# In each unit of a fused attention: the scores of the next unit first, the maxima of five units ahead behind them

## The reference

```python
mod = silu(c) @ w_ada + b_ada                     # six vectors: shift, scale, gate, twice
h = norm(x) * (1 + scale) + shift
q, k, v = split(h @ w_qkv + b_qkv)                # 16 heads of 9 dimensions
attn = softmax(q @ k.T / sqrt(9))                 # 128 x 128 for each head and sequence
x = x + gate * (attn @ v @ w_proj + b_proj)
x = x + gate2 * mlp(norm(x) * (1 + scale2) + shift2)
```

## Time and profile before

| | |
|---|---|
| three runs | 1516.69, 1521.12, 1522.37 us |
| profiled execution | 1514.8 us, span of the trace 1512.9 us |
| mean granted TensorE clock | 0.977 |
| L648, maxima (x2048) | 122.2 us busy, 53.8 us idle before it |
| L666 and L670, scores (x4096) | 331.5 us busy, 3.5 us idle before them |
| L1259, exponential (x256) | 262.4 us busy, 1025 ns each |
| L1567, reduction (x256) | 310.8 us busy, 1214 ns each, 90.4 us idle before it |

### The profile page before, as it was taken

The page is one execution under the profiler, slowest core; times in us unless marked ns, Lnnn a source line. Parts: engine busy times, 40 slices in busy tenths (PEclk is TensorE's granted clock), DMA queues, the critical chain, the costliest instruction groups (busy, mean ns, idle before and its releaser), DMA issues. The chain is left out here.

```text
span 1512.9 us, 41073 instructions
## 1 busy us (share of the span) xinstructions
PE 1400.6 (93%) x16016; PEld 1047.5 (69%) x16016; DVE 1022.3 (68%) x2537; ACT 780.3 (52%) x1290; POOL 570.0 (38%) x771
## 2 busy tenths in 40 slices
PE   5799998999999999999998878887999999998998
PEld 2377776777777776777776666665776677676776
DVE  4688885766776767888546698886446666665342
ACT  2377764333333336776645466665554455564543
POOL 3355542211131213554324455653425243433222
PEclk9799999999999999999999999999999999998999
DMA  4755641111122033555000443453216766674111
GB/s 128 160 152 150 163 103 54 52 45 45 37 61 76 9 106 80 147 145 135 18 32 25 123 106 90 119 124 88 47 28 104 112 107 126 129 123 92 33 48 48
DMA packets 209129, 134.94 MB, mean 89 GB/s; under 512 B 142461, under 2 KB 191320, under 8 KB 202730
## 3 DMA queue, kind: packets, MB, share of 16 engines
q1 hardware_dynamic: 188978, 129.74, 35.7%
q10 hardware_dynamic: 19960, 2.57, 1.2%
HBM read 98.24 MB, written 33.24 MB: 87 GB/s over the span
## 5 line engine op out<-in xcount | busy, mean ns | idle before, releaser
L1567 DVE TENSOR_REDUCE negm<-banks 128x8 bf16<-128x1024 f32 x256 | 310.8, 1214 | 90.4 <-PE banks L648 89.5
L1259 ACT ACTIVATE prob<-banks 128x1024 f32<-128x1024 f32 x256 | 262.4, 1025 | 147.1 <-PE banks L670 143.8
L2031 POOL TENSOR_TENSOR X<-X,gx 128x288 f32<-128x288 f32 x128 | 104.1, 826 | 261.7 <-DVE gx L1597 259.9
L1393 ACT ACTIVATE hid<-banks 128x512 f32<-128x512 f32 x144 | 85.9, 597 | 219.9 <-PE banks L960 219.9
L976 PEld LDWEIGHTS banks<-wfc,hid 128*128 128x128 f32 x1152 | 156.7, 190 | 32.3 <-issue 20.1
L648 PE MATMUL banks<-qk 54*128 54x128 bf16 (+1 forms) x2048 | 122.2, 240 | 53.8 <-DVE negm L1567 23.0
L666 PE MATMUL banks<-qk 54*128 54x128 bf16 (+1 forms) x2048 | 167.4, 234 | 3.5 <-ACT prob L1259 1.7
L670 PE MATMUL banks<-mT,identb 64*128 64x128 bf16 x2048 | 164.1, 223 | 0.0
L976 PE MATMUL banks<-wfc,hid 128*128 128x144 f32 x1152 | 161.6, 286 | 2.1 <-DVE hid L1767 2.1
L648 PEld LDWEIGHTS banks<-qk 54*128 54x128 bf16 (+1 forms) x2048 | 69.6, 101 | 128.4 <-issue 68.5
L959 PE MATMUL banks<-hT,wfc 128*128 128x512 f32 x288 | 148.6, 597 | 1.0 <-DVE hid L1479 0.5
(11 more groups left out here) (172 smaller groups left out, 2778.5 us busy)
## 6 DMA issues: line engine op xcount, KB each, us to landing
qk<-qk_scr SPq DMA_DIRECT2D x96, 216.0 KB
gbuf<-gate_scr SPq DMA_DIRECT2D x64, 288.0 KB, 4.5
qk_scr<-parts SPq DMA_DIRECT2D x48, 288.0 KB, 2.8
qk<-qk_scr SPq DMA_DIRECT2D x96, 144.0 KB
qk<-cw_scr SPq DMA_DIRECT2D x8, 1024.0 KB, 4.9
qk_scr<-parts SPq DMA_DIRECT2D x48, 144.0 KB, 2.4
qk<-qk_scr SPq DMA_DIRECT2D x96, 72.0 KB
qk<-tok_scr SPq DMA_DIRECT2D x32, 216.0 KB
```

The lines of the kernel that those rows point to most:

```text
L1259: act.activation(prob[:, 2 * (U % 3):2 * (U % 3) + 2, :], pairs[1][:], ACT.Exp, scale=scale).then_inc(a_exp, 1)
L1567: dve.tensor_reduce(negm[:, u // 2, :, 4 * (u % 2):4 * (u % 2) + 4], pairs[0][:].rearrange("q s (h k) -> q s h k", k=T), AX.X, ALU.max, ne ...
```

## The change

In every unit of the attention the call of `scores(l, U + 1)` now stands ahead of `scores_for_max(l, U + AHEAD)`. The opening of a layer (`start_layer` and the units that the MLP issues) is as it was, and so is every other engine's program.

```diff
                     for u in range(UNITS):
                         U = UNITS * n + u
+                        if U + 1 < last:
+                            scores(l, U + 1)
                         if U + AHEAD < last:
                             scores_for_max(l, U + AHEAD)
-                        if U + 1 < last:
-                            scores(l, U + 1)
                         if u % 2 == 1 and U + 3 < last:
```

## The result

The changed kernel takes 1513.61 us in the median of 22 runs (1501.99 to 1521.99), the kernel before 1520.45 us in as many (1510.81 to 1531.23). The ratio is 0.9943 with a 95% interval of 0.9925 to 0.9961: 8.7 us faster, 5.9 to 11.4 (the medians differ by 6.8 us, the means by 8.1). The forecast was 3.6 us faster, 1517.5 us, range 1507 to 1525. The time lies in the range; the gain is about twice the forecast one.

What follows compares the result with a forecast made beforehand. TensorE, busy 93% of the span, was taken as the bound, so only its waits or slowed time could be won. +4.0 - 3.9 - 2.3 - 1.4 = -3.6 us, from the 1521.12 us median to 1517.5, range 1507 to 1525.

Steps and rivals of the forecast that it cites:

- The split into chains: TensorE's waits: maxima to maxima gain nothing; landing or other part to maxima shrink, maxima to other part grow, up to 0.56 us.
- Rival 1: All layers: every wait ahead of the maxima is hidden, -16 us, 1505 us; chance 0.15.
- Rival 3: Late maxima lose 6.7 us in layers 0 and 1 and 3.4 in layer 2, no gain: +10, 1531 us; chance 0.08.
- Rival 4: Whole kernel: the reordering does nothing anywhere, 1521 us; chance 0.10.
- Layers 0 and 1: forecast +4.0 us: Late unit 4 maxima delay a group's head transpose, 6.7 us lost; DMA waits return 1.4 and 1.3.
- the term of 12 x 0.56 = 6.7: Layers 0 and 1: twelve groups without slack each lose 0.56 us at the transpose waiting for GpSimd's copy.
- Layer 2: forecast -3.9: Scores run inside unit 3's DMA waits: six groups 0.56 us shorter each, 3.4, and 0.5 in the first group.
- clock term: Layer 2: shorter DMA waits may remove two clock drops of 1.4 us each; half counted, -1.4 us.
- The direct term: Layer 2: the gain from shorter DMA waits without the clock, 0.56 us a group, -3.9 us in all.
- Layer 3: forecast -2.3: Four DMA waits ahead of the maxima each shrink by up to 0.82 us: 0.8 from the longest, 1.5 from the others.
- The wait term: Layer 3: the gain from four shorter DMA waits, -2.3 us, with no clock drops counted.
- Rival 2: The clock decides: all four drops after waits vanish, -5.6 instead of -1.4 us, 1513 us; chance 0.12.

Runs made afterwards that it cites:

- e6_only6: Scores ahead of the maxima only in unit 6 of each group, against the kernel before: 1521.82 us, ratio 1.0007 (0.9985 to 1.0030).
- e5_only4: Scores ahead of the maxima only in unit 4 of each group, against the kernel before: 1525.94 us, ratio 1.0035 (1.0014 to 1.0055).
- e1_layers01: Scores ahead of the maxima only in layers 0 and 1, against the kernel before: 1522.86 us, ratio 1.0013 (0.9995 to 1.0030).
- e3_unit3: Scores ahead of the maxima only in unit 3 of each group, against the kernel before: 1515.10 us, ratio 0.9957 (0.9935 to 0.9980).
- e2_layers23: Scores ahead of the maxima only in layers 2 and 3, against the kernel before: 1511.98 us, ratio 0.9934 (0.9912 to 0.9956).
- e9_whole: The whole change once more, against the kernel before on the same chip: 1511.50 us, ratio 0.9956 (0.9936 to 0.9976).
- e7_best: Scores first everywhere but in unit 4 of layers 0 and 1, against the kernel before: 1511.43 us, ratio 0.9951 (0.9929 to 0.9972).

## Why the prediction was right, and what was mis-sized

**The split into chains held.** A wait between two groups of maxima gives nothing (e6_only6; in unit 6 it is there in both orders, 0.42 and 0.32 us from start to start), a chain from the maxima to another part of the stream costs (e5_only4, e1_layers01), one from a landing to the maxima gives (e3_unit3's 6.79 us for 7.26). Rival 1, every wait hidden, is refused by e1_layers01 and e6_only6. Rival 3, slower, came true only as its first half, in layers 0 and 1. Rival 4 is out by the interval. That the total fell inside the range is in part luck: the terms missed by -2, +1.5 and -4 us.

**Layers 0 and 1: forecast +4.0 us, measured +2.0 (e1_layers01; -0.8 to +4.6), by the stages 2.8 - 0.7.** The lateness is 0.47 us and not 0.56, and a group grows by 0.37 to 0.40 us (22.47 to 22.84 in layer 0, 22.30 to 22.70 in layer 1), since VectorE makes up some 0.08 of it. So the term of 12 x 0.56 = 6.7 measures about 4.6. In layer 1 that is paid back in full in these traces: its second group, which has a DMA wait of 0.73 us before, is 0.7 to 1.3 us shorter after, its end up to 0.95. I had 1.3 for both. How much of it is the change is not shown: in e2_layers23, which has the maxima first there, that second group takes 22.6 us too, as with the whole change, and not 23.8.

**Layer 2: forecast -3.9, with its clock term -5.3, measured -3.8.** The direct term is 0.46 us for each landing, at most 6 x 0.46 = 2.8; with the first group, 0.6 us shorter in both traces of the whole change, 3.4 of the 3.9. The clock term of 1.4 is not to be found in the sum, though its drops moved: before, two of the landings have a drop behind them, besides the last, which has one in both orders; in the two traces of the whole change only the last has. From such a landing to the next maxima it takes 1.4 us more (4.67 against 3.28, rows 8). After, drops come behind L696 instead, ahead of the landing, where a wait for the DMA can absorb them. The clock loses more in this layer than before (14.5 against 11.4 us in the mean) and the layer is shorter all the same. That fits time lost before a landing costing nothing until the DMA wait is used up; no run isolates it.

**Layer 3: forecast -2.3, measured -6.4. This is where the sum was mis-sized, and by its clock term.** The wait term held: unit 3 alone gives 1.7 us (224.9 against 226.6, e3_unit3) at the same clock, and TensorE's idle time in this layer's attention falls from 7.4 to 5.3 us in the mean of the first two columns. In it is a wait that I had read as one between maxima and hence worth nothing, the 1.17 us at the layer's opening. The maxima that its chain starts at are issued with the MLP ahead of the layer, which the change leaves as it was, so by my own rule it had to shrink; without a drop in either, the stretch from the layer's first scores to L581 takes 5.96 us with the maxima first (e3_unit3, e6_only6) and 5.40 with the scores first.

The other 4 us and more are drops of the clock, for which I had counted nothing here. In all three traces of the first column the clock loses 13.7 us in this layer, in the four of the second 5.1 to 8.5, in the mean 7.2: between three and four drops fewer. A drop costs less than the 1.7 us of full speed that it takes: a group with one and without a wait takes 29.59 us and one with neither 28.32 (from one L581 to the next, the second group of the layer, before and e9_whole), 1.3 us, elsewhere up to 1.5. So the drops are worth 4 to 5 us. Why they became fewer is not shown. At the opening the drop is behind the wait in four of six traces. One of twice the length stood behind the longest DMA wait (4.4 us); that wait is 0.19 us in the trace after, but another of 2.6 us stands in the group ahead of it, with a drop behind it, and in e9_whole it is 2.0 us with a drop. Most of the others come at the end of a group, where hardly anything waits. And fewer drops alone don't make the layer shorter: e6_only6 loses 10.2 us there and takes 227.1, with 10.6 us of idle time.

**The clock term: forecast -1.4 in layer 2, found in layer 3.** Rival 2 said that all drops behind waits vanish, 1513 us. The time came out there, but not for its reason: in layer 2 and behind the longest waits drops are still there, and the mean granted clock over all runs of e9_whole (0.9726) is that of its kernel before (0.9724), so no clock was gained in sum. By the table, drops are fewer in layer 3, where TensorE sets the pace in most groups, and more frequent in layer 2, where a DMA does. The Trainium skill (TensorE: Matmul & The Clock Gate, HAM oscillation) says that waits between short bursts throttle the array again and again. The opening of layer 3 agrees in four traces of six, 0.50 behind 1.17 us, and not in the other two, 1.00 behind the same wait; nor does the wait of 1.35 us at 1022.54 with 1.00 behind it.

## What to carry to other kernels

Before moving a call in an in-order stream, write down for each wait where its chain starts: if it starts at the same call one turn earlier, hiding it yields nothing, and what is queued behind the call in another engine's chain comes later by what was put in front. A wait that an unmoved chain will refill (L581 here) makes a good place to check the loss. A chain that starts at a call outside the changed loop, as at a layer's opening, counts as unmoved. And try the exception: with the one unit left out whose maxima head the long chain, the groups of layers 0 and 1 are back at 22.3 to 22.4 us, and the whole took 1508 to 1509 us in two runs and 1511 in the third (e7_best), against 1511.5 and 1513.6 for the whole change.

A single profiled execution can be several us off the median of its kernel (spans of 1512.9 and 1519.6 us for the same one). Compare stage by stage, with the lost clock beside each stage, and read a wait from start to start where the row ahead of it has changed.

## What the runs showed of the hardware

Before, the eight small matmuls of the maxima take 0.23 us up to the scores behind them, and the sixteen of the scores 0.56 us up to the transposes L690. After, the scores take 0.47 us up to the maxima and the maxima 0.33 up to L690 (126.22, 126.69 and 127.02 above). The sum is 0.79 in both orders. Inside them a pair starts every 0.06 us in either order; the step from the last pair is 0.05 us where the other of the two follows and 0.15 where L690 or L655 does. So the 0.1 us belongs to the step out of these matmuls, and the call that stands last pays it.

Over many executions the time goes with the granted clock in both orders. With the scores first the correlation is -0.72 (22 executions); with the maxima first it is -0.16, -0.69 and -0.54 in three series (29, 35 and 13 executions). So these numbers don't show that one order hides clock drops better than the other.
